# Attention steps moved in a fused attention and mixture-of-experts kernel: reciprocals' division, values' and Q's projections, norm, rank and split at other steps

## The chip, the cores and the metric

The kernel runs on one core of a Trainium2 chip. The metric is the device time of one execution in microseconds, the median of several. Engines are named as in the profile: PE (TensorE, with PEld for its weight loads), DVE (VectorE), ACT (ScalarE), POOL (GpSimd), SP (SyncE, which only issues DMAs here).

## The reference

Input x is 16 batches of 512 tokens with 256 channels.

```python
q, k, v = heads(wq, bq), heads(wk, bk), heads(wv, bv)     # 16 heads of 16
q, k = rope(q), rope(k)
att = softmax(causal(q @ k.T * 0.25))
x = layernorm(x + (att @ v) @ wp.T + bp)
probs = softmax(x @ gate_w.T)                              # 32 experts
top_w, top_idx = top_k(probs, 8); top_w /= top_w.sum()
y = sum over chosen e of top_w[e] * ((u * silu(g)) @ down_w[e].T),  g, u = split(x @ gate_up_w[e].T)
out = layernorm(x + y)
```

## The kernel before

It has two phases. In the attention phase the main loop runs over i, the batch (0 to 15), and e, a step (0 to 31). Eight steps are one group of four heads; k = e % 8 is the place in the group. At each step PE computes two scores (`score`, lines 1075 and 1077: keys by queries, then a mask), ACT takes their exponentials (`exp`), and PE multiplies these with the values at odd steps (`pv`, line 1089). Beside this run, at steps that the table `SLOT_...` gives, three other jobs:

- For batch i + 1: transposes of x, projections of Q, K and values (`p1_qk`, line 1024; `p1_v`, line 1035), rope on DVE (line 1634) and its rotation (`rotate`, 1641 and 1642), and the split of Q and K into three bfloat16 parts: ACT copies a part (`part_copy`, tile pbuf), DVE subtracts (`rest`, 1650; `last_part`, 1657). ACT puts the values into vx (`values`). SP writes the parts to DRAM and loads them back in other order (tile stacks).
- For the group after next: row maxima of the scores. PE computes them in eleven units (`max_unit`, 1049 and 1051), at the (k, place) pairs of `PLACES`, and DVE reduces each (`reduce_unit`, 1664).
- For batch i - 1, its end: SP fetches the softmax sums (tile den), DVE takes reciprocals, SP writes them out (step 6) and reads them back broadcast over 16 rows (`reciprocals_in`, step 10, tile xTden) after the numerators (step 9, tile ynum; it waits for the rotation of K). DVE divides (`divide`, 1927), PE projects (`project`, 1100 and 1102, steps 15 and 16), DVE adds (1818) and takes statistics (1825, 1828; steps 16 and 17). GpSimd computes the inverse root (`rsqrt`, 872 and 874), DVE the mean column (1835), ACT the norm (tile x), GpSimd stores it (878). Then transposes, router, choice, ranks, and GpSimd's scatter of batch i - 2's rows (888) by expert, 32 per batch at steps 0 to 19.

Each step of PE has three places for such jobs: 0 after the first score, 1 and 2 after the second and `pv`. Every engine works through its own queue in the order that this loop writes; semaphores tie the queues. All jobs with an output in PSUM outside scores share four banks in turn (`odd_plan` and the class `Odd`): a job waits until the reader of the job four before it is done. `odd_plan` repeats the loop to number them, which is why the change touches both.

In the second phase PE computes the experts (152 steps k, two blocks of 256 rows each), ACT and DVE copy the results, and GpSimd scatters them to token order (`rows_to_tokens`, 906, four per step; buffers for seven blocks). The end of batch 15 runs at the same step numbers of this phase, so `SLOT_RSQRT` and others apply there too. GpSimd also scatters the rows of batches 14 and 15 (888). DVE sums each token's eight rows at the end.

Of the kernel before, what the change touches and what calls it, by code (L numbers as in the profile page):

```python
# [37 lines left out]

SLOT_X = (0, 1)
SLOT_Q = (2, 3)  # L40
SLOT_V = (5, 7)
SLOT_K = (6, 7)
SLOT_X_OUT = (0, 1)
SLOT_ROPE_Q = (2, 3)
SLOT_ROPE_K = (6, 7)
SLOT_VALUES = (5, 6)
SLOT_ROTATE = (3, 7)
SLOT_FIRST = (4, 9)
SLOT_REST = (4, 9)
SLOT_SECOND = (5, 10)  # L50
SLOT_LAST = (5, 11)
SLOT_WRITE = (7, 12)
SLOT_DEN = 2
SLOT_RECIP = 4
SLOT_REC_OUT = 6
SLOT_REC_IN = 10
SLOT_NUM = 9
SLOT_DIVIDE = 12
SLOT_PROJECT = (15, 16)
SLOT_ADD = (15, 16)  # L60
SLOT_STATS = (16, 17)
SLOT_RSQRT = 20
SLOT_MEAN = 20
SLOT_NORM = 22
SLOT_STORE = 21
SLOT_X1 = (24, 25)
SLOT_X1_OUT = (24, 25)
SLOT_SPLIT = 26
SLOT_LOWER = 29
SLOT_ROUTER = 26  # L70
SLOT_ROUTER_IN = 26
SLOT_CHOICE = (26, 27)
SLOT_MASK = 27
SLOT_RANK = 28
SLOT_RANK_IN = 28
SLOT_EXP = 28
SLOT_RESIDUAL = 0
SCATTER_STEPS = 20
SLOT_WEIGHTS = 31
SLOT_TABLE = 10  # L80
SLOT_TABLE_OUT = 25
SLOT_TAILS = 27

STEPS = 32
LE = STEPS // NQ

PLACES = [(4, 0), (5, 1), (6, 0), (6, 2), (7, 0), (7, 1), (7, 2), (0, 1), (1, 0), (1, 1), (1, 2)]
MSLOT = {at: m for m, at in enumerate(PLACES)}
MHALF = 4
SPLIT, TURN, TURN_OUT, ROWS_K = (1, 2), (3, 2), 3, 4  # L90
# [183 lines left out]
def odd_plan():  # L274

    bank, at = {}, [0]

    def take(i, *job):
        bank[job] = 6 if i >= B else 3 + at[0] % 4
        at[0] += 1  # L280
    for kc in range(NC):
        take(0, "x", 0, kc)
    for n in range(2):
        for half in range(2):
            take(0, "qk", 0, n, half)
    for v in range(2):
        take(0, "v", 0, v)
    for m in range(NM):
        take(0, "max", 0, m)
    take(0, "turn", 0)  # L290
    for m, (k, place) in enumerate(PLACES):
        if k >= MHALF:
            take(0, "max", 1, m)
    for i in range(B + 2):
        for e in range(STEPS):
            g, k = e // LE, e % LE
            end, nxt = 1 <= i <= B, i <= B - 2
            for place in range(3):
                if place == 0 and e == SLOT_TABLE_OUT and table_of(i - 1):
                    take(i, "table", i - 1)  # L300
                if place == 1:
                    if e in SLOT_X and nxt:
                        take(i, "x", i + 1, SLOT_X.index(e))
                    if e in SLOT_Q and nxt:
                        take(i, "qk", i + 1, 0, SLOT_Q.index(e))
                    if e in SLOT_K and nxt:
                        take(i, "qk", i + 1, 1, SLOT_K.index(e))
                    if e in SLOT_V and nxt:
                        take(i, "v", i + 1, SLOT_V.index(e))
                    if e in SLOT_PROJECT and end:  # L310
                        take(i, "project", i - 1, SLOT_PROJECT.index(e))
                    if e in SLOT_X1 and end:
                        take(i, "x1", i - 1, SLOT_X1.index(e))
                    if e == SLOT_ROUTER and end:
                        take(i, "router", i - 1)
                if place == 2 and e == SLOT_RANK and end:
                    take(i, "rank", i - 1)
                n = max_group(i, e)
                if n is not None:
                    if (k, place) in MSLOT:  # L320
                        take(i, "max", n, MSLOT[k, place])
                    if (k, place) == TURN:
                        take(i, "turn", n)
            if prep_step(i, e):
                stage, p = prep_step(i, e)
                if p + E * stage in range(1, E + 1):
                    take(i, "gu", p + E * stage - 1)
                    take(i, "dn", p + E * stage - 1)
                if stage == 1 and p in (2, 3):
                    take(i, "fin", p - 2)  # L330
    return bank
# [9 lines left out]
def build(nc, x, wq, bq, wk, bk, wv, bv, wp, bp, gate_w, gate_up_w, down_w,  # L341
# [9 lines left out]
    with ExitStack() as ctx:  # L351
# [601 lines left out]
        def _(pe):  # L953
# [59 lines left out]
            def p1_transpose(b, kc):  # L1013
                wait(pe, s_xin, 16 * (b + 1))
                k = odd.take(s_xT, 2 * b + kc + 1, "x", b, kc)
                xpose4(k, lambda n: xin[:, n, kc * P:(kc + 1) * P]).then_inc(s_p1t, 1)

            def p1_qk(b, n, half):

                wait(pe, s_xT, 2 * b + 2)  # L1020
                w = (wqT, wkT)[n]
                k = odd.take(s_rope, 8 * b + 4 * n + 2 * half + 2, "qk", b, n, half)
                for kc in range(NC):
                    last = mmul(ps[:, k, :], w[:, kc, half * P:(half + 1) * P], xTden[:, kc, :],  # L1024
                                start=(kc == 0), stop=(kc == NC - 1))
                last.then_inc(s_p1q, 1)

            def p1_v(b, v):

                wait(pe, s_xT, 2 * b + 2)  # L1030
                k = odd.take(s_vx, 2 * b + v + 1, "v", b, v)
                for m in range(2):
                    t = 2 * v + m
                    for kc in range(NC):
                        last = mmul(ps[:, k, m * C:(m + 1) * C], xTden[:, kc, t * P:(t + 1) * P], wvT[:, kc, :],
                                    start=(kc == 0), stop=(kc == NC - 1))
                last.then_inc(s_p1v, 1)
# [68 lines left out]
            def x1_transpose(b, kc):  # L1106
                wait(pe, s_x1, NT * (b + 1))
                k = odd.take(s_x1T, 2 * b + kc + 1, "x1", b, kc)
                xpose4(k, lambda n: x1[:, n, kc * P:(kc + 1) * P]).then_inc(s_x1t, 1)
# [104 lines left out]
            def odd_job(i, e, place):  # L1214

                end, nxt = has(i, 1, NB), has(i, 0, NB - 2)
                if place == 0 and e == SLOT_TABLE_OUT:
                    for t in table_of(i - 1):
                        table_transpose(t)
                if place == 1:  # L1220
                    if e in SLOT_X and nxt:
                        p1_transpose(i + 1, SLOT_X.index(e))
                    if e in SLOT_Q and nxt:
                        p1_qk(i + 1, 0, SLOT_Q.index(e))
                    if e in SLOT_K and nxt:
                        p1_qk(i + 1, 1, SLOT_K.index(e))
                    if e in SLOT_V and nxt:
                        p1_v(i + 1, SLOT_V.index(e))
                    if e in SLOT_PROJECT and end:
                        project(i - 1, SLOT_PROJECT.index(e))  # L1230
                    if e in SLOT_X1 and end:
                        x1_transpose(i - 1, SLOT_X1.index(e))
                    if e == SLOT_ROUTER and end:
                        router(i - 1)
                if place == 2 and e == SLOT_RANK and end:
                    rank(i - 1)

                k, n = e % LE, max_group(i, e)
                if n is not None:
                    if (k, place) in MSLOT:  # L1240
                        max_unit(n, MSLOT[k, place])
                    if (k, place) == TURN:
                        max_transpose(n)
# [303 lines left out]
        def _(dve):  # L1547
# [133 lines left out]
            def router_in(b):  # L1681
                wait(dve, s_gt, b + 1)
                V.tensor_copy(lg[:, :, :], ps[:, odd_bank("router", b), 0:NT * E].rearrange("p (t e) -> p t e", t=NT)).then_inc(s_rt, 1)
# [262 lines left out]
            def odd_job(i, e, place):  # L1946

                end, nxt = has(i, 1, NB), has(i, 0, NB - 2)
                if place == 0 and e == SLOT_TABLE_OUT:
                    for t in table_of(i - 1):  # L1950
                        table_out(t)
                if place == 1:
                    if e in SLOT_ROPE_Q and nxt:
                        rope(i + 1, 0, SLOT_ROPE_Q.index(e))
                    if e in SLOT_ROPE_K and nxt:
                        rope(i + 1, 1, SLOT_ROPE_K.index(e))
                    if e in SLOT_ADD and end:
                        ln_add(i - 1, SLOT_ADD.index(e))
                    if e == SLOT_ROUTER_IN and end:
                        router_in(i - 1)  # L1960
                if place == 2 and e == SLOT_RANK_IN and end:
                    rank_in(i - 1)
                k, n = e % LE, max_group(i, e)
                if n is not None:
                    if (k, place) in MSLOT:
                        reduce_unit(n, MSLOT[k, place])
                    if (k, place) == SPLIT:
                        split_max(n)
# [131 lines left out]
```

## Time and profile before

| | us |
|---|---|
| median of 3 runs | 2179.51 (2176.76 to 2180.5) |
| profiled execution | 2177.83 |
| its span | 2175.9 |
| PE busy | 1805.7 (83%) |
| DVE busy | 1601.1 (74%) |
| ACT busy | 1356.5 (62%) |
| POOL busy | 1245.6 (57%) |

Busy shares are means over two phases with different limits, so they say little by themselves. The issue time of DMAs is not in them. A row with an idle time in brackets says how long the engine stood before that instruction and what ended it.

### The profile page before, as it was taken

The page shows a single profiled execution, that of the slowest core. Times are in us where ns is not written, and L with a number is a line of the kernel's source. Part 1 is how long each engine was busy: PE and PEld are TensorE (multiplying, and loading weights), DVE is VectorE, ACT ScalarE, POOL GpSimd, SP SyncE. Part 2 cuts the span into 40 slices and gives each one's busy share as a digit, 9 for nine tenths or more (in the row PEclk, how much of TensorE's full clock was granted, in tenths as well). Part 3 has the DMA queues.
Part 4 walks back from the last instruction along what each step waited for, and adds up shares of the span by engine and source line. Part 5 has one row for each costly group of instructions (what it writes and reads, how often), then busy time and mean ns, then how long its engine had stood idle before and what let it go on. Part 6 is the DMA issues. An engine that isn't in the chain of part 4 may idle for free.

```text
span 2175.9 us, 54014 instructions
## 1 busy us (share of the span) xinstructions
PE 1805.7 (83%) x17104; PEld 1295.0 (60%) x17104; DVE 1601.1 (74%) x3572; ACT 1356.5 (62%) x3265; POOL 1245.6 (57%) x1206
## 2 busy tenths in 40 slices
PE   4899888998888888988878988899888889988920
PEld 2555554555555544555445877788777678777820
DVE  4888787877888778877864545475456677778988
ACT  1657565666565555555445867788777678888820
POOL 1004356444644465445543777777777777777860
PEclk8999999999999999999988999999999999999965
DMA  5456567666756766566676765656689889989977
GB/s 142 120 153 196 190 215 228 199 199 209 235 184 198 254 212 204 172 192 210 197 228 235 243 201 189 204 191 211 201 299 299 304 295 308 300 285 356 356 237 251
DMA packets 242891, 495.04 MB, mean 228 GB/s; under 512 B 47800, under 2 KB 140415, under 8 KB 232848
## 3 DMA queue, kind: packets, MB, share of 16 engines
q1 hardware_dynamic: 158720, 299.30, 44.4%
q0 software_dynamic: 58368, 163.70, 20.4%
q10 hardware_dynamic: 25536, 28.58, 3.9%
q8 instruction: 155, 2.54, 0.5%
q14 instruction: 112, 0.92, 0.1%
HBM read 284.54 MB, written 234.04 MB: 238 GB/s over the span
## 4 chain that ended last, share of the span: by engine, by line
PE 40%; DVE 19%; DMA 14%; issue 11%; ACT 7%; POOL 5%; SPq 2%; ACTq 1%; POOLq 0%; DVEq 0%
DMA xTden<-reciprocals 6%; DVE mn L1664 5%; PE ps L1024 4%; POOL y_tokens L906 4%; PE ps L1102 3%; DMA y_tokens<-work,yidx 3%; PE ps L1049 3%; PE ps L1163 3%; PE ps L1075 3%; PE ps L1143 3%; PE ps L1145 3%; PE ps L1144 3%; PE ps L1089 3%; PE ps L1209 2%; PE ps L973 2%
## 5 line engine op out<-in xcount | busy, mean ns | idle before, releaser
L1301 ACT ACTIVATE pT<-ps 128x512 f32<-128x512 f32 (+2 forms) x1008 | 677.7, 703 | 381.8 <-PE ps L1077 292.6
L888 POOL DMA_INDIRECT x_sorted<-xhl,idx x512 | 529.2, 1034 | 483.6 <-DVE xhl L1739 229.4
L1664 DVE TENSOR_REDUCE mn<-ps 128x1 f32<-128x512 f32 (+3 forms) x704 | 412.9, 632 | 51.0 <-PE ps L1051 48.6
L1143 PE MATMUL ps<-pT,gu_hi 128*128 128x256 f16 (+1 forms) x1600 | 371.0, 251 | 43.2 <-ACT pT L1301 43.0
L1144 PE MATMUL ps<-pT,gu_hi 128*128 128x256 f16 (+1 forms) x1600 | 370.0, 250 | 0.0
L1145 PE MATMUL ps<-pT,gu_lo 128*128 128x256 f16 (+1 forms) x1600 | 369.7, 250 | 0.0
L906 POOL DMA_INDIRECT y_tokens<-work,yidx x264 | 279.5, 1059 | 79.8 <-issue 61.2
L1049 PE MATMUL ps<-stacks 96*128 96x512 bf16 (+3 forms) x1024 | 273.8, 310 | 42.5 <-DVE mn L1664 25.6
L1075 PE MATMUL ps<-stacks 99*128 99x512 bf16 (+3 forms) x1024 | 283.7, 308 | 15.4 <-ACT pT L1301 12.3
L1077 PE MATMUL ps<-maskk,identb 128*128 128x128 bf16 x1024 | 221.8, 222 | 0.0
L1209 PE MATMUL ps<-dn,vx 128*128 x608 | 168.5, 277 | 53.2 <-DVE cosT L1872 15.5
L1051 PE MATMUL ps<-maskq,identb 128*128 128x128 bf16 x1024 | 198.5, 224 | 0.0
L1089 PE MATMUL ps<-pT,vx 128*32 128x512 f32 (+3 forms) x2048 | 195.5, 454 | 2.8 <-ACT pT L1301 2.6
L1143 PEld LDWEIGHTS ps<-pT,gu_hi 128*128 x1600 | 158.2, 99 | 64.9 <-issue 52.0
L1049 PEld LDWEIGHTS ps<-stacks 96*128 96x128 bf16 x1024 | 102.3, 100 | 129.2 <-DVE mn L1664 50.1
L1858 DVE TENSOR_TENSOR vx<-vx 128x512 f16<-128x512 f32 x152 | 105.0, 691 | 99.8 <-ACT vx L1301 98.6
L1211 PE MATMUL ps<-dn,vx 128*128 x608 | 169.2, 278 | 0.0
L1210 PE MATMUL ps<-dn,vx 128*128 x608 | 168.9, 278 | 0.0
L1145 PEld LDWEIGHTS ps<-pT,gu_lo 128*128 x1600 | 158.3, 99 | 11.4
L1144 PEld LDWEIGHTS ps<-pT,gu_hi 128*128 x1600 | 158.6, 99 | 7.6
L1075 PEld LDWEIGHTS ps<-stacks 99*128 99x128 bf16 x1024 | 102.5, 100 | 101.2 <-ACT pT L1301 26.2
L1853 DVE SCALAR_TENSOR_TENSOR vx<-vx,ps 128x512 f32<-128x512 f32 x152 | 103.8, 683 | 61.8 <-PE ps L1145 60.0
(255 smaller groups left out, 3899.3 us busy)
## 6 DMA issues: line engine op xcount, KB each, us to landing
stacks<-y_tokens SPq DMA_DIRECT2D x64, 1024.0 KB
stacks<-qk_parts SPq DMA_DIRECT2D x128, 192.0 KB
qk_parts<-pbuf SPq DMA_DIRECT2D x31, 768.0 KB, 4.4
stacks<-qk_parts SPq DMA_DIRECT2D x128, 128.0 KB
attention<-yev ACTq DMA_DIRECT2D x64, 256.0 KB
stacks<-x_sorted SPq DMA_DIRECT2D x52, 304.0 KB, 4.2
x_sorted<-pads_h SPq DMA_DIRECT2D x99, 152.0 KB
pbuf<-x_sorted SPq DMA_DIRECT2D x40, 304.0 KB
```

What stands on the lines that cost most here:

```text
L888: pool.indirect_dma_start(xsort[g][:, :], bass.IndirectOffsetOnAxis(ap=at, axis=0), xhl_rows[:, t, :], None).then_inc(s_scat, 16)
L906: pool.indirect_dma_start(ytok[g][:, :], bass.IndirectOffsetOnAxis(ap=yidx[:, c:c + 1], axis=0), ysb[n % NYR][:, m, :].bitcast(I32), None, ...
L1049: mmul(ps[:, k, a * n:(a + 1) * n], qs[0:KS, r, h, tt * P:(tt + 1) * P], ks[0:KS, r, h, 0:n], start=True, stop=False)
L1075: mmul(ps[:, o, at:at + n], ks[0:KX, r, h, s * P:(s + 1) * P], qs[0:KX, r, h, s * P:T], start=True, stop=False)
L1077: last = mmul(ps[:, o, at:at + P], identb[:, :], maskk[:, :], start=False, stop=True)
L1089: last = mmul(ps[32 * j:32 * j + 32, BANK_PV, s * P:T], value_columns(i % 2, s, 4 * g + j), pT[s % 2][:, j, 0:T - s * P], start=(s == 0), ...
L1143: mmul(o, w_hi[k], x_hi[k], start=k == 0, stop=False)
L1144: mmul(o, w_hi[k], x_lo[k], start=False, stop=False)
L1145: last = mmul(o, w_lo[k], x_hi[k], start=False, stop=k == n - 1)
L1209: mmul(o, h_hi, d_hi, start=True, stop=False)
L1301: return nc.scalar.activation(o, i, f, **k)
L1664: V.tensor_reduce(mn[:, tt, h0:h0 + nh], ps[:, odd_bank("max", at, m), 0:nh * n].rearrange("p (a n) -> p a n", a=nh), axis=AX.X, op=ALU.ma ...
```

## The change

It changes step numbers (`SLOT_...`), adds a place within the step for each of the jobs of PE and of their readers on DVE (`PLACE_...`, where before all had place 1 and rank had 2), and moves one maximum unit from (5, 1) to (5, 0). No instruction is added or removed.

```diff
-SLOT_V = (5, 7)
+SLOT_V = (6, 8)
-SLOT_VALUES = (5, 6)
+SLOT_VALUES = (5, 8)
-SLOT_FIRST = (4, 9)
+SLOT_FIRST = (4, 8)
-SLOT_DEN = 2
+SLOT_DEN = 1
-SLOT_DIVIDE = 12
+SLOT_DIVIDE = 13
-SLOT_RSQRT = 20
+SLOT_RSQRT = 16
-SLOT_STORE = 21
+SLOT_STORE = 20
-SLOT_SPLIT = 26
+SLOT_SPLIT = 28
-SLOT_RANK = 28
-SLOT_RANK_IN = 28
+SLOT_RANK = 29
+SLOT_RANK_IN = 29
+PLACE_X = (1, 1)
+PLACE_Q = (0, 0)
+PLACE_V = (0, 0)
+PLACE_K = (1, 1)
+PLACE_ROPE_Q = (0, 1)
+PLACE_ROPE_K = (1, 1)
+PLACE_PROJECT = (1, 1)
+PLACE_ADD = (1, 1)
+PLACE_X1 = (1, 1)
+PLACE_ROUTER = 1
+PLACE_ROUTER_IN = 1
+PLACE_RANK = 0
+PLACE_RANK_IN = 0
-SLOT_TAILS = 27
+SLOT_TAILS = 26
+def due(e, place, slots, places):
+    return e in slots and place == places[slots.index(e)]
-PLACES = [(4, 0), (5, 1), (6, 0), (6, 2), (7, 0), (7, 1), (7, 2), (0, 1), (1, 0), (1, 1), (1, 2)]
+PLACES = [(4, 0), (5, 0), (6, 0), (6, 2), (7, 0), (7, 1), (7, 2), (0, 1), (1, 0), (1, 1), (1, 2)]
```

In `odd_plan` and in `odd_job` of PE and DVE each test changes in the same manner, for example:

```diff
-                if place == 1:
-                    if e in SLOT_Q and nxt:
-                        p1_qk(i + 1, 0, SLOT_Q.index(e))
+                if due(e, place, SLOT_Q, PLACE_Q) and nxt:
+                    p1_qk(i + 1, 0, SLOT_Q.index(e))
-                if place == 2 and e == SLOT_RANK and end:
+                if (e, place) == (SLOT_RANK, PLACE_RANK) and end:
                     rank(i - 1)
```

## Rows read from the trace of the kernel before

**Rows 1.** Of the page: busy time of each engine; TensorE's granted clock in 40 slices.
```profile
PE 1805.7 (83%) x17104; PEld 1295.0 (60%) x17104; DVE 1601.1 (74%) x3572; ACT 1356.5 (62%) x3265; POOL 1245.6 (57%) x1206
...
PEclk8999999999999999999988999999999999999965
```

**Rows 2.** All waits: who waited for whom; us in total, times, longest.
```profile
PE ps L1100 <- DVE mn L1664: 45.3, 15, 7.5
...
DVE ynum L1927 <- DMA xTden<-reciprocals: 40.6, 15, 8.1
...
ACT vx L1301 <- PE ps L1035: 86.9, 15, 5.8
...
DVE tiny L1835 <- POOL tiny L874: 18.8, 7, 13.0
...
PE ps L973 <- ACT work L1301: 26.0, 17, 1.9
...
PE ps L1024 <- DVE mn L1664: 10.1, 17, 0.9
```

**Rows 3.** Chain that ended last, 498 to 514 us (batch 6): start, us, what.
```profile
497.98 0.61 DVE qf L1642
...
500.63 0.57 SPq L714
...
501.25 9.21 DMA xTden<-reciprocals
...
511.78 0.61 DVE mn L1664
```

**Rows 4.** Timeline, batch 6, 480 to 530 us: start, us, engine, line, operation [idle before].
```profile
484.09 0.75 DVE L1634 SCALAR_TENSOR_TENSOR qf<-ps,bqc,cosT 128x512 f32<-128x512 f32 x1 [0.94 <-PE ps L1024]
...
489.28 1.06 ACT L1301 ACTIVATE pbuf<-qf 128x1024 bf16<-128x1024 f32 x1 [0.39 <-DVE qf L1650]
...
494.21 1.89 PE L1035 MATMUL ps<-wvT,xTden 128*128 128x256 f32 x8
...
496.36 1.02 DVE L1664 TENSOR_REDUCE mn<-ps 128x1 f32<-128x384 f32 x2 [0.39 <-PE ps L1051]
...
510.49 1.29 DVE L1927 TENSOR_TENSOR ynum<-ynum,xTden 128x512 f32<-128x512 f32 x2 [2.92 <-DMA xTden<-reciprocals]
```

**Rows 5.** First projection: TensorE's timeline in batches 3 and 6; windows of line 1102.
```profile
296.35 0.27 PE L1100 MATMUL ps<-spare,ones 65*128 65x256 bf16 x1 [1.78 <-DVE mn L1664]
...
296.46 1.03 PE L1102 MATMUL ps<-wpT,ynum 128*128 128x256 f32 x4
...
512.53 0.37 PE L1100 MATMUL ps<-spare,ones 65*128 65x256 bf16 x1 [2.37 <-DVE mn L1664]
...
512.69 1.92 PE L1102 MATMUL ps<-wpT,ynum 128*128 128x256 f32 x4
...
152.60:156.60 4.00, 2.96 (x12) 2.11 (x13) 1.00 0.60 149
...
512.60:516.60 4.00, 3.60 (x8) 2.33 (x8) 0.58 0.71 228
```

**Rows 6.** Timeline of GpSimd and VectorE, batch 6, at the norm.
```profile
520.03 0.97 POOL L888 DMA_INDIRECT x_sorted<-xhl,idx  x1 [0.49 <-PE ps L1077]
...
524.74 0.25 DVE L1828 BATCH_NORM_AGGREGATE mv<-st 128x2 f32<-128x6 f32 x2
...
525.73 0.19 POOL L872 TENSOR_SCALAR tiny<-mv 128x4 f32<-128x4 f32 x1
```

**Rows 7.** Experts' phase: GpSimd's largest group, 1185 to 2110 us; timelines 1276 to 1312.
```profile
L906 POOL DMA_INDIRECT y_tokens<-work,yidx x264 | 279.5, 1059 | 79.8 <-issue 61.2
...
1279.09 0.25 DVE L1828 BATCH_NORM_AGGREGATE mv<-st 128x2 f32<-128x6 f32 x2
...
1282.89 0.97 POOL L888 DMA_INDIRECT x_sorted<-xhl,idx  x1 [0.30 <-issue]
...
1308.74 0.16 DVE L1835 SCALAR_TENSOR_TENSOR tiny<-mv,tiny 128x4 f32<-128x4 f32 x1 [12.99 <-POOL tiny L874]
```

More of the change, by code:

```diff
@@ L300, in odd_plan @@
                     take(i, "table", i - 1)
-                if place == 1:
-                    if e in SLOT_X and nxt:
-                        take(i, "x", i + 1, SLOT_X.index(e))
-                    if e in SLOT_Q and nxt:
[L305 to L315, printed above, removed]
-                if place == 2 and e == SLOT_RANK and end:
+                if due(e, place, SLOT_X, PLACE_X) and nxt:
+                    take(i, "x", i + 1, SLOT_X.index(e))
+                if due(e, place, SLOT_Q, PLACE_Q) and nxt:
+                    take(i, "qk", i + 1, 0, SLOT_Q.index(e))
+                if due(e, place, SLOT_K, PLACE_K) and nxt:
+                    take(i, "qk", i + 1, 1, SLOT_K.index(e))
+                if due(e, place, SLOT_V, PLACE_V) and nxt:
+                    take(i, "v", i + 1, SLOT_V.index(e))
+                if due(e, place, SLOT_PROJECT, PLACE_PROJECT) and end:
+                    take(i, "project", i - 1, SLOT_PROJECT.index(e))
+                if due(e, place, SLOT_X1, PLACE_X1) and end:
+                    take(i, "x1", i - 1, SLOT_X1.index(e))
+                if (e, place) == (SLOT_ROUTER, PLACE_ROUTER) and end:
+                    take(i, "router", i - 1)
+                if (e, place) == (SLOT_RANK, PLACE_RANK) and end:
                     take(i, "rank", i - 1)
@@ L1219, in odd_job @@
                         table_transpose(t)
[L1220 to L1223, printed above, removed]
-                        p1_qk(i + 1, 0, SLOT_Q.index(e))
[L1225 to L1235, printed above, removed]
+                if due(e, place, SLOT_X, PLACE_X) and nxt:
+                    p1_transpose(i + 1, SLOT_X.index(e))
+                if due(e, place, SLOT_Q, PLACE_Q) and nxt:
+                    p1_qk(i + 1, 0, SLOT_Q.index(e))
+                if due(e, place, SLOT_K, PLACE_K) and nxt:
+                    p1_qk(i + 1, 1, SLOT_K.index(e))
+                if due(e, place, SLOT_V, PLACE_V) and nxt:
+                    p1_v(i + 1, SLOT_V.index(e))
+                if due(e, place, SLOT_PROJECT, PLACE_PROJECT) and end:
+                    project(i - 1, SLOT_PROJECT.index(e))
+                if due(e, place, SLOT_X1, PLACE_X1) and end:
+                    x1_transpose(i - 1, SLOT_X1.index(e))
+                if (e, place) == (SLOT_ROUTER, PLACE_ROUTER) and end:
+                    router(i - 1)
+                if (e, place) == (SLOT_RANK, PLACE_RANK) and end:
                     rank(i - 1)
@@ L1951, in odd_job @@
                         table_out(t)
[L1952 to L1961, printed above, removed]
+                if due(e, place, SLOT_ROPE_Q, PLACE_ROPE_Q) and nxt:
+                    rope(i + 1, 0, SLOT_ROPE_Q.index(e))
+                if due(e, place, SLOT_ROPE_K, PLACE_ROPE_K) and nxt:
+                    rope(i + 1, 1, SLOT_ROPE_K.index(e))
+                if due(e, place, SLOT_ADD, PLACE_ADD) and end:
+                    ln_add(i - 1, SLOT_ADD.index(e))
+                if (e, place) == (SLOT_ROUTER_IN, PLACE_ROUTER_IN) and end:
+                    router_in(i - 1)
+                if (e, place) == (SLOT_RANK_IN, PLACE_RANK_IN) and end:
                     rank_in(i - 1)
```

## The prediction

> **What bounds the kernel now.** I read the page first: TensorE is busy 83% of the span and its clock falls to half again and again [rows 1]. Two phases follow from the slices: sixteen attention batches up to about 1170 us, then the experts. Next I read the waits. In attention the longest wait of TensorE is one place, the first projection of a batch (line 1100), 45.3 us in 15 times, 3.0 us each; VectorE waits 40.6 us for the broadcast reciprocals just before it [rows 2]. Then the chain of waits over one batch: the rotation of K ends at 498.6, SyncE issues numerators and reciprocals, the reciprocals' DMA takes 9.21 us, the two divisions follow, then one maximum of 0.61 us, and only then the projection starts at 512.53 [rows 3 to 5]. So an attention batch is paced by this chain: rotation, DMA, division, projection.
>
> The experts' phase has another bound. Its GpSimd scatter of results takes 1.06 us each with 0.30 us before it, 608 of them and 63 row scatters, without a hole from 1183 to 2107 (the largest group is in [rows 7]): 264 take 279.5 + 79.8 us, so 1.36 us each, and 608 of them at that price are 827 us, the row scatters some 80 more. What other engines lose there costs nothing while GpSimd is busy.
>
> **The change part by part.** Nothing is added or removed; instructions change their place in each queue. The times are of the profiled execution, 2177.8 us (its span 2175.9 and 1.9 around it); the median of the runs shown is 1.7 above it.
>
> Division from step 12 to the end of 13. TensorE's first projection (step 15) needs both the division and the maximum of step 13, whose bank it takes. Before, VectorE waits 2.92 us for the DMA, divides, and does that maximum last (0.61 us, [rows 3, 4]). After, the maximum lies in the wait, since its matmuls are done early (they move to place 0 of step 5 of each group as well), and the division comes last. Gain: one maximum a batch, 15 x 0.61 = 9 us. Where there is no DMA wait (batches 8 and 14, which compute tables) the sum of the two is the same and the gain is nothing, so 13 to 15 times: 8 to 9 us. Nothing behind the division suffers: the maxima of step 14 are needed only after the projection, which takes over 2 us.
>
> Values' projection. Its second half moves from step 7, behind K's second half and ahead of two maxima, to step 8. Before, VectorE idles 0.39 us for the maxima behind the 1.89 us of matmul, and these stand ahead of K's rotation [rows 4]. That 0.39 goes. ScalarE, which sat up to 5.8 us for this half (86.9 us in all, [rows 2]), no longer does; but that idle time hid nothing that TensorE waited for, as TensorE ran its own queue meanwhile, so I give it nothing. The first half moves behind a maximum and a score, so it ends some 0.4 us later.
>
> Q's projection to place 0 of steps 2 and 3. The second half then runs ahead of a score and of a product with the values. VectorE idles 0.94 us before that rope [rows 4] and starts sooner by at most that. But ScalarE copies the second part of Q (489.28, [rows 4]) behind the evacuation of the values' first half, which is now later by 0.4; before, it left 0.39 idle there. So of 0.94 about 0.2 arrives. Together K's rotation ends 0.4 to 0.7 us sooner. How much of this reaches the division depends on the DMA: between 0 and 0.7, and I take 0.4, since stack loads of the same queue still run when the numerators are issued. Fourteen batches: 6 us (0 to 10).
>
> At this place a rule of the Trainium skill speaks against the change. The page "DMA: Bandwidth & Descriptors", section "Queues, rings and completion order", says that each engine consumes descriptors of one queue in ring order, so that what is issued sooner on SyncE's queue still stands behind the stack loads issued ahead of it. By that rule the landing moves only as the loads do, 0.2 us a batch, and this term would be 3 us and not 6. The row shows only that the DMA takes 9.21 us from the last issue, not what it stands behind [rows 3].
>
> The clock. When TensorE has waited for the projection, the next matmuls run at the lower level: 1.92 us for four in batch 6, after 2.37 us of waiting, against 1.03 in batch 3, which had waited 1.78 us only [rows 5]. Of the 15 windows laid from each first projection over 4 us, 13 have a mean granted clock of 0.50 to 0.64 and two have 1.00 (the first and the sixth are in [rows 5]); one of the two is the batch that had waited 1.78 us. Four matmuls lose 0.9 us; the eight of this projection lose at most 1.8 and, as the clock came back within them, some 1.6 us. If the wait shrinks by 1.0 us (0.6 + 0.4), the batches that waited 2.1 to 2.4 us, five of them by the timeline (batch 6 is the row), come near the 1.8 that kept the clock. I take four that keep it: 4 x 1.6 = 6 us (0 to 13 x 1.6 = 21).
>
> Norm: rsqrt on GpSimd from step 20 to 16. The scatters of steps 17 to 19, four of them, now stand behind its wait for the statistics. In batch 6 GpSimd is at step 17's scatter near 520 and the statistics end at 525.0 [rows 6]; so GpSimd idles over 5 us and the four scatters (0.97 us and 0.30 ahead of each) end near 532, instead of 525.7. Their reader is the split, which moves from 26 to 28, some 5 us behind that, and the store stands at 20, behind the norm; the slack covers both. If it did not, a late split costs up to 1 us a batch. The mean column waits for rsqrt 5.8 us in seven late batches (of 18.8 us, the other 13.0 lies in the experts' phase, [rows 2, 7]); this goes. I take half as passed on: 3 us (0 to 6).
>
> Rank moves by a score (0.2 us), VectorE's ropes and ScalarE's early copy of K's part by a step, all with their producers: 0, bounds -3 to +3 us from the shortest waits near them. The softmax sums' fetch at step 1 instead of 2 gives nothing: SyncE has nothing between, and it waits for ScalarE's store at its own step 2. The table's tails move by one step: nothing waits.
>
> Experts' phase. There rsqrt at 20 holds VectorE 12.99 us (1308.74, [rows 7]). The statistics are ready at 1279.34. GpSimd would reach step 16 at about 1284, behind the row scatter of step 15 at 1282.89, so it doesn't wait, and VectorE's 13 us go. But GpSimd was busy through them, and it bounds this phase: gain 0 to 1 us, a loss up to 3 if the store at 20 must wait for the norm at 22. I take 0.
>
> Sum: 9 + 6 + 6 + 3 + 0 = 24 us. 2177.8 - 24 = 2153.8, and at the level of the median 2155.
>
> **The rivals.** (B) Only the reordering counts: the DMA lands as before and the clock stays low. Gain 9 us, 2170. For it: the loads on the same queue; by the rule above it would be a little more, 2168. Against: VectorE's and the loads' start move too. Chance 0.17.
>
> (C) The wait goes altogether: TensorE's projection wait of 45.3 us and the low clock behind it, 13 x 1.6 = 21 us, less what other waits take over (a third): 66 x 2/3 = 44 us, 2135, at the full 66 us 2113. For it: batch 3, with a wait of 1.8 us, kept its clock. Against: my gain of 1.0 us is a third of the mean wait. Chance 0.15.
>
> (D) The gain turns into another wait, within 0.2% of before: 2178. For it: TensorE waits 26.0 us in 17 times for scaled weights, and 10.1 for maxima [rows 2]; a sooner start meets these. Chance 0.11.
>
> (E) Slower. The early copy of K's part (1.06 us for one such copy, [rows 4]) with the values' evacuation now stands on ScalarE ahead of the exponentials of step 9, and the score of step 10 needs one of these. I work out that it is ready some 0.9 us after TensorE comes there. This decides if TensorE's time up to the projection, not the chain, ends last: then it is 0.9 x 15 = 13 us on top, 2191. Against: 3.0 us of waiting at the projection absorb it. Chance 0.10.
>
> The forecast itself has 0.47. Its own range is 2143 to 2168. The range for 8 in 10 reaches into (C) and to the edge of (D): 2122 to 2180. A difference of 0.2%, 4.4 us, is about what runs can tell. Faster: 0.47 + 0.17 + 0.15 = 0.79, less 0.02 for (B) at its end: 0.77; same 0.13; slower 0.10.
>
> **What would show it.** Right: the maximum of step 13 stands ahead of the division and the projection follows the division within 0.2 us; line 1100's wait falls from 45.3 to about 30 us; more of the 15 windows have a clock near 1.00; ScalarE's wait for the values' projection nearly vanishes; VectorE's 13 us in the experts' phase vanish and that phase keeps its length. Wrong: the reciprocals' DMA grows by what its issue gains (B); a new wait of 0.9 us at the score of step 10 without a fall at line 1100 (E); the split waits for scatters; the wait at line 1100 is gone in most batches (C).

## The result: 25 us faster, most of what the traces show ahead of the first projection

| us | before | after |
|---|---|---|
| median (lowest to highest, runs) | 2178.14 (2166.42 to 2180.5, 4) | 2153.03 (2144.49 to 2157.7, 4) |
| profiled execution | 2177.83 | 2157.70 |
| its span | 2175.9 | 2155.8 |

The ratio is 0.9891, its 95% interval 0.9843 to 0.9938. Lines of the code stand 17 or 18 further down in the kernel after: the projection of lines 1100 and 1102 is at 1118 and 1120, the maximum at 1681, the division at 1944, rsqrt at 890 and 892, the mean column at 1852, and the row scatter at 906 (a number that `rows_to_tokens` had before).

The page of the kernel after, with the rows that answer to [rows 1]:

```profile
PE 1812.3 (84%) x17104; PEld 1297.4 (60%) x17104; DVE 1598.4 (74%) x3572; ACT 1364.2 (63%) x3265; POOL 1243.9 (58%) x1206
...
PEclk8999999999999999999989999999999999999965
```

The busy times moved by less than 8 us each; the time went out of idle stretches. The windows of the two phases say in which phase. Columns: the stretch, its length, busy time with counts of PE, PEld, DVE, ACT and POOL, then the mean clock. Kernel before (first score of batch 1 is at 115.9, last score at 1172.5):

```profile
60.00:1172.50 1112.50, 974.31 (x7841) 576.86 (x7838) 890.58 (x2158) 635.65 (x1241) 509.06 (x507) 0.95 0.62 199
1172.50:2108.40 935.90, 800.74 (x9125) 698.47 (x9123) 623.10 (x1233) 706.99 (x2004) 721.27 (x686) 0.96 0.79 265
```

Kernel after, the same two phases:

```profile
58.90:1154.90 1096.00, 976.93 (x7871) 578.25 (x7869) 891.52 (x2164) 645.47 (x1246) 508.78 (x507) 0.95 0.63 203
1154.90:2089.80 934.90, 805.66 (x9125) 701.49 (x9123) 624.04 (x1235) 707.92 (x2005) 720.38 (x687) 0.96 0.79 265
```

The last score of attention comes 17.6 us sooner, the experts' phase is 1.0 shorter, the sums behind it 1.5. In attention the mean clock has not moved, and neither have the busy times, but for ScalarE's, which is 10 us longer.

The waits of the kernel after, the rows that answer to [rows 2]:

```profile
POOL tiny L890 <- DVE mv L1845: 121.7, 15, 42.4
DVE ynum L1944 <- DMA xTden<-reciprocals: 38.1, 12, 7.8
PE ps L1118 <- issue: 37.7, 12, 7.0
PE ps L991 <- ACT work L1318: 25.8, 17, 1.9
ACT vx L1318 <- PE ps L1053: 15.7, 15, 1.2
...
DVE tiny L1852 <- POOL tiny L892: 3.4, 6, 1.4
PE ps L1042 <- DVE mn L1681: 3.4, 15, 0.6
PE ps L1118 <- DVE ynum L1944: 2.8, 2, 1.7
```

The wait at the projection is now in two rows, 37.7 + 2.8 = 40.5 us; it was 45.3. TensorE's wait at K's banks (line 1042, before 1024) went from 10.1 to 3.4, ScalarE's for the values from 86.9 to 15.7, the mean column's from 18.8 to 3.4. GpSimd now waits at rsqrt, 121.7 us: 42.4 of it once, in batch 1, where it stood 43.3 us before as well, and some 5.5 us in each later batch.

The chain of the last end does not pass through batch 6 in this execution, so I show the same stretch by the timeline, as [rows 4 and 5] did for before. Batch 6 begins (first score) at 472.9 before and at 471.6 after, 1.3 us sooner:

```profile
494.93 0.68 DVE L1658 TENSOR_TENSOR qf<-qf,ynum 128x512 f32<-128x512 f32 x1
495.53 0.68 DVE L1659 TENSOR_TENSOR qf<-qf,ynum 128x512 f32<-128x512 f32 x1
...
496.24 1.34 SPq L739 DMA_DIRECT2D ynum<-attention  x2
497.74 2.15 SPq L732 DMA_DIRECT2D xTden<-reciprocals  x2
...
504.86 1.31 DVE L1681 TENSOR_REDUCE mn<-ps 128x1 f32<-128x512 f32 x2 [0.23 <-PE ps L1069]
...
509.01 1.29 DVE L1944 TENSOR_TENSOR ynum<-ynum,xTden 128x512 f32<-128x512 f32 x2 [2.84 <-DMA xTden<-reciprocals]
510.23 1.74 DVE L1681 TENSOR_REDUCE mn<-ps 128x1 f32<-128x512 f32 x3
...
510.41 0.27 PE L1118 MATMUL ps<-spare,ones 65*128 65x256 bf16 x1 [2.10 <-issue]
```

From the start of the division to the projection it is now 1.40 us, where it was 2.04 (510.49 to 512.53, [rows 4, 5]): the maximum of 0.61 us no longer stands between. The rotation of K ends at 24.6 us of the batch, not 25.7.

For the whole phase I worked the same distances out of one trace of each run, as means over batches 1 to 15 in us from the batch's first score (the rotation over 14); e1 to e12 are the experiments below. "Issued" is the end of the last of the four issues of numerators and reciprocals on SyncE, "rest" runs from the projection's first weighted matmul to the next batch, "low" is the time in us in these batches at the lower of the two clock levels.

```
               rotation issued division projection rest   low
before          25.61   28.35   36.78    39.10    31.34   102
e1              25.61   28.31   36.93    38.46    31.44    85
e3              25.61   28.29   36.78    39.08    31.33    99
e2              24.39   27.23   36.07    38.36    31.08    96
after           24.39   27.37   36.30    37.89    31.31   102
e10 (= after)   24.38   27.15   36.05    37.58    30.96    82
e4              24.69   27.51   36.29    37.81    30.93    79
e11 (= e4)      24.69   27.52   36.35    37.88    31.07    89
e5              25.15   27.94   36.51    38.03    30.73    61
e8              24.39   27.26   36.14    38.16    29.90    48
e9              24.69   27.57   36.39    38.33    30.08    58
e6              24.38   26.03   35.52    37.05    30.31    58
e12             24.39   25.91   35.67    37.82    30.07    48
e7              24.39   25.58   33.94    35.67    29.94    44
```

Before to after: the projection comes 1.21 us sooner, times 15 is 18 us; the rest and the low time are the same. That is the whole 17.6 us of the phase (batch 1 begins 1.0 later). A second trace of the kernel after (e10) has the projection 1.52 us and the rest 0.38 us shorter than before, so one pair of traces fixes these differences only to some 0.3 us a batch.

### The profile page after: what moved, and what is told of

The parts are those of the page before. It is cut to its first block and busy times, and to the rows that moved or that the text cites. A ratio compares the mean times of both kernels' runs of the same rounds, so it can differ in the third digit from the quotient of the medians.

```text
span 2155.8 us, 54014 instructions
## 1 busy us (share of the span) xinstructions
PE 1812.3 (84%) x17104; PEld 1297.4 (60%) x17104; DVE 1598.4 (74%) x3572; ACT 1364.2 (63%) x3265; POOL 1243.9 (58%) x1206
## 5 line engine op out<-in xcount | busy, mean ns | idle before, releaser
L1681 DVE TENSOR_REDUCE mn<-ps 128x1 f32<-128x512 f32 (+3 forms) x704 | 415.0, 632 | 45.3 <-PE ps L1069 42.9
L1093 PE MATMUL ps<-stacks 99*128 99x512 bf16 (+3 forms) x1024 | 295.3, 308 | 11.5 <-ACT pT L1318 6.8
L1163 PEld LDWEIGHTS ps<-pT,gu_lo 128*128 x1600 | 159.0, 99 | 11.2
```

The source lines that it names most:

```text
L1093: mmul(ps[:, o, at:at + n], ks[0:KX, r, h, s * P:(s + 1) * P], qs[0:KX, r, h, s * P:T], start=True, stop=False)
L1163: last = mmul(o, w_lo[k], x_hi[k], start=False, stop=k == n - 1)
L1681: V.tensor_reduce(mn[:, tt, h0:h0 + nh], ps[:, odd_bank("max", at, m), 0:nh * n].rearrange("p (a n) -> p a n", a=nh), axis=AX.X, op=ALU.ma ...
```

## The experiments

Theory 1: an attention batch is paced by rotation of K, issue on SyncE, DMA of the reciprocals, division, projection. Theory 2, the rival: TensorE's other waits, which the moved projections of Q and values shorten, are what the change saved. The clock was a question of its own. Three groups ran on a chip each, with the kernel before beside them: e1 to e4; e5, e7, e8 and e9; e6, e10, e11 and e12. The medians of before there: 2180.32 (20 runs), 2178.63 (11), 2177.91 (11). Behind each median stand its range and number of runs, then the ratio to before with its 95% interval.

**e1, the division alone**, in the kernel before:

```diff
-SLOT_DIVIDE = 12
+SLOT_DIVIDE = 13
```

> The kernel before with the division at step 13 and nothing else. Theory 1 (the chain rotation, DMA, division, projection paces a batch): the maximum of step 13 goes into the DMA wait, 0.6 us a batch, 8 to 9 us faster than before, about 2169. Theory 2 (the gain of the change comes from waits of TensorE for exponentials and for K's bank, which went down by 12 us in the trace after, and the projection's wait is only what is left over): no change, within 3 us of before.

Measured: 2168.26 (2161.78 to 2175.19, 9); 0.9949, 0.9931 to 0.9967. 12 us. The distance from division to projection falls by the table from 2.32 to 1.53 us, 15 times 0.8 = 12. In this trace the division itself starts 0.15 us later, so the projection comes 0.64 us sooner, 10 us in all, and batches 1 to 15 take 8 us less. The prediction's largest term is shown, at 8 to 12 where it said 9. The wait at the projection, in the waits of e1:

```profile
PE ps L1100 <- issue: 35.1, 13, 7.0
```

**e2, the change without the division's move:**

```diff
-SLOT_DIVIDE = 13
+SLOT_DIVIDE = 12
```

> The kernel after with the division back at step 12. Theory 1: 8 to 9 us slower than after, about 2162. Theory 2: the time of after, 2153, within 3 us.

Measured: 2160.42 (2156.47 to 2166.23, 6); 0.9908, 0.9887 to 0.9929: 7 us behind the kernel after. That compares two chips; by the ratios to before the edit is worth 2 to 4 us (0.9891 and 0.9898 against 0.9908). By the table the projection is 0.47 us later than in the kernel after, 7 us in all. So from this side the division is worth 2 to 7 us, from e1 it was 8 to 12: its gain is shown, its size only roughly, and the 9 lies between. The wait at the projection has its old releaser again, in the waits of e2:

```profile
PE ps L1118 <- DVE mn L1681: 46.6, 16, 7.0
DVE ynum L1944 <- DMA xTden<-reciprocals: 44.5, 15, 7.7
```

The same run says what all the other parts are worth together: 20 us against before on the same chip (2180.32 to 2160.42), of which the table has 11 in the earlier projection and 4 in the shorter rest. From e1 to the kernel after, which differ by the same parts, it is 13 to 15 us (2168.26 to 2155.48, that is e10, or 2153.03). The prediction had 6 + 6 + 3 = 15 for them.

**e3, the norm's steps alone**, in the kernel before:

```diff
-SLOT_RSQRT = 20
+SLOT_RSQRT = 16
-SLOT_STORE = 21
+SLOT_STORE = 20
-SLOT_SPLIT = 26
+SLOT_SPLIT = 28
```

> The kernel before with rsqrt at 16, store at 20 and split at 28 alone. Theory 1: the chain does not hold it, so 1 to 3 us faster than before (the store's wait of 0.8 us and part of 5.8 us of VectorE's waits); VectorE's wait of 13.0 us in the experts' phase goes and gives nothing there, as GpSimd is without a hole. Rival: that wait was on the path, then 10 to 13 us faster. If the scatters behind rsqrt come late for the split: slower by up to 15 us.

Measured: 2177.01 (2170.43 to 2181.3, 12); 0.9985, 0.997 to 1.0. That is 3 us, with an interval that ends at none; the profiled execution shows no gain in attention (the table). VectorE's 13 us at the mean column are gone here too, in the waits of e3:

```profile
DVE tiny L1835 <- POOL tiny L874: 3.4, 6, 1.4
```

So that gap was not worth the 10 to 13 us of the rival; at most it is part of these 3 us, and the interval ends at 7.

**e4, the change with the values' projection as it was:**

```diff
-SLOT_V = (6, 8)
+SLOT_V = (5, 7)
-SLOT_VALUES = (5, 8)
+SLOT_VALUES = (5, 6)
-SLOT_FIRST = (4, 8)
+SLOT_FIRST = (4, 9)
-PLACE_V = (0, 0)
+PLACE_V = (1, 1)
-PLACES = [(4, 0), (5, 0), ...
+PLACES = [(4, 0), (5, 1), ...
```

> The kernel after with the values' projection, its evacuation, the copy of K's part and the maximum unit back at their old steps; division, Q and norm stay moved. Theory 1: K's rotation ends about 0.5 us later in the batch, 5 to 9 us slower than after, about 2160. Theory 2: the waits for exponentials at steps 11 and 13 and for K's bank come back, 12 us slower, about 2165, and the projection's wait falls by as much as those rise.

Measured: 2141.73 (2136.61 to 2157.55, 6); 0.9833, 0.9801 to 0.9865. Not slower, as both theories had it, but 11 us ahead of the kernel after. ScalarE's long wait is back and costs nothing:

```profile
ACT vx L1318 <- PE ps L1053: 99.2, 30, 6.0
```

TensorE's waits for exponentials rise too, by 8.4 us. The rotation is only 0.3 us later (the table). I took the 11 us as a question of spread, since the kernel after had been timed on another chip, and ran both again as e10 and e11.

**e5, the change with Q's projection as it was:**

```diff
-PLACE_Q = (0, 0)
+PLACE_Q = (1, 1)
-PLACE_ROPE_Q = (0, 1)
+PLACE_ROPE_Q = (1, 1)
```

> The kernel after with Q's projection and its rope back at place 1; all else as after. Theory 1: 0.94 us of VectorE's idle time comes back, of which 0.2 us a batch reaches K's rotation: 0 to 3 us slower than after. Theory 3 (Q's earlier place is what brings K's rotation forward by 1.0 us in the batch, as it came 0.8 us earlier still with the values' projection at its old steps): rotation 0.8 us later in each batch and 8 to 12 us slower than after.

Measured: 2152.8 (2143.64 to 2159.39, 6); 0.9876, 0.9843 to 0.9909: the time of the kernel after. TensorE's wait at K's banks is back at 9.6 us, and so is the idle time before Q's rope (first row; second, the later rotation), in e5's batch 6, which begins at 467.5:

```profile
478.73 0.75 DVE L1651 SCALAR_TENSOR_TENSOR qf<-ps,bqc,cosT 128x512 f32<-128x512 f32 x1 [0.92 <-PE ps L1042]
...
491.44 0.68 DVE L1658 TENSOR_TENSOR qf<-qf,ynum 128x512 f32<-128x512 f32 x1
```

By the table the rotation is 0.76 us later, the division only 0.2 to 0.5 and the projection 0.1 to 0.45 (against after and e10), so 2 to 7 us were to be lost; the spread of the runs covers that. A low time of 61 us in this execution goes the other way. So this run neither shows a loss nor excludes one of that size.

**e7, the reciprocals' DMAs (two a batch) taken out of the kernel after.** It leaves the normalisation by the softmax sums out: nothing is loaded into xTden and the division doesn't wait for it.

```diff
-                for c in range(NC):
-                    src = rec_dram[b][8 * c:8 * c + 8, :].rearrange("h (o t) -> h o t", o=1).to_broadcast([8, D, T])
-                    sp.dma_start(xTden[:, c, :], src).then_inc(s_yd, 16)
...
-                wait(dve, s_yd, 64 * (b + 1))
+                wait(dve, s_yd, 32 * (b + 1))
```

> The kernel after without the broadcast of the reciprocals to tile xTden: SyncE does not issue it, the division waits for the numerators alone and multiplies by what lies in xTden, so that the attention's result is not normalised (left out: 2 DMAs a batch). Theory 1: the projection's wait of 40 us and the low clock behind it go, 35 to 60 us faster than after, about 2105. Rival (the wait is cover for the maxima, VectorE ends last): under 15 us faster, 2140.

Measured: 2105.04 (2104.66 to 2107.33, 4); 0.9661, 0.9628 to 0.9694. 48 us ahead of the kernel after. In its batch 6 the division has no idle time before it (first fence), and in the whole run it waits for the numerators once, in batch 15 (second fence, of the waits):

```profile
491.26 1.28 DVE L1941 TENSOR_TENSOR ynum<-ynum,xTden 128x512 f32<-128x512 f32 x2
```

```profile
DVE ynum L1941 <- DMA ynum<-attention: 3.3, 1, 3.3
PE ps L1115 <- DVE ynum L1941: 2.9, 2, 1.7
```

This settles the bound: the broadcast of the reciprocals holds 48 of the 2153 us. By the table the earlier projection is 29 to 33 us of it and the shorter rest, with a low time of 44 us, 15 to 21; what follows attention is the same within 2 us. The four runs also lie within 2.7 us of each other, where those of the kernel after span 13 to 15. That suggests that the spread comes with this wait; four runs don't show it.

**e8, sixteen idle matmuls ahead of the projection's wait**, in the kernel after, so that TensorE is not at rest there:

```diff
+FILL = 16
...
+                k = odd.take(s_ln1, LN * b + v + 1, "project", b, v)
+                for f in range(FILL if v == 0 else 0):
+                    mmul(ps[:, k, 0:C], ones[0:65, :], biasp[0:65, :], start=True, stop=True)
                 wait(pe, s_yn, 2 * b + 2)
-                k = odd.take(s_ln1, LN * b + v + 1, "project", b, v)
```

> The kernel after with 16 idle matmuls (65 rows, 256 columns, 0.11 us each, overwritten by the projection) at the first projection of each batch, ahead of the wait for the division. Clock theory: TensorE's clock no longer falls there in most batches, 1.6 us a batch in 13 batches less 1.7 us in the three batches without a long wait: 10 to 18 us faster than after, about 2140. Rival (the fall of the clock is not set by this wait but by what went before it, so the filler changes nothing of it): 0 to 5 us slower than after.

Measured: 2148.1 (2145.29 to 2152.52, 4); 0.986, 0.9825 to 0.9895. 5 us ahead of the kernel after (standard error 2.4), fewer than expected. The clock did what it should: ten of the 15 windows at the first projection have 1.00, where the kernel after has two and e10 four, and the four matmuls behind the fill take 1.03 us, those of the kernel after took 1.07 and then 1.91. In e8, batch 6 (which begins at 464.5):

```profile
501.18 1.92 PE L1117 MATMUL ps<-spare,ones 65*128 65x256 bf16 x16
501.62 1.29 DVE L1947 TENSOR_TENSOR ynum<-ynum,xTden 128x512 f32<-128x512 f32 x2 [2.51 <-DMA xTden<-reciprocals]
...
503.10 1.03 PE L1123 MATMUL ps<-wpT,ynum 128*128 128x256 f32 x4
```

In the kernel after, batch 6:

```profile
510.52 1.07 PE L1120 MATMUL ps<-wpT,ynum 128*128 128x256 f32 x4
...
511.59 1.91 PE L1120 MATMUL ps<-wpT,ynum 128*128 128x256 f32 x4
```

By the table the low time falls from 82 to 102 us to 48 and the rest of a batch from 31.0 to 31.3 us to 29.9, some 16 to 21 us in all. But the distance from division to projection grows from 1.5 to 2.0 us (7 us), since TensorE is often still in the fill when the division is done; the projection is 0.3 to 0.6 us later in the batch (4 to 9 us). And the profiled execution of the kernel after that had the lower low time (e10) needs only 7 us more in these batches (1028.1 against 1021.0).

**e9, e4 with the fill of e8:**

> The kernel with the values' projection back at its old steps (2141.7 us measured) and the same 16 idle matmuls. Clock theory: the difference between that kernel and after, 11 us, is the clock (its trace has 78 us at the low level in batches 1 to 15, after has 102); with the filler both kernels come to the same time within 4 us, about 2135. Rival (it is the order of the work that makes the difference): the 11 us stay between them, 2130 against 2140 or 2142 against 2153.

Measured: 2146.23 (2136.94 to 2150.51, 5); 0.9832, 0.9801 to 0.9863. It comes within 2 us of e8, as the clock theory had it, though both at 2147 and not at 2135. It is also within the spread of e4: the fill and the values' old place do not add up.

**e10, the kernel after once more, and e11, e4 once more**, on one chip:

> The kernel after itself, on the same chip as the next three, since the kernels were so far compared over different chips. It should come to 2153 (ratio 0.989) within its interval; what the next three are worth is read against this one.

> The kernel after with the values' projection at its old steps, once more. If the 11 us that it was ahead of after are real (the move of the values' projection costs): 8 to 14 us faster than after on this chip. If they are the spread of the clock between executions (the rotation of K is only 0.3 us later in its batches and the first projection starts at the same place): within 5 us of after, either way.

Measured: e10 2155.48 (2143.84 to 2159.23, 6); 0.9898, 0.9875 to 0.9921. e11 2151.4 (2144.96 to 2156.03, 6); 0.9874, 0.985 to 0.9898. The 11 us shrink to 4, with intervals that overlap. All 10 runs of the kernel after have the mean 2153.2 (standard error 1.8), all 12 with the values back 2147.8 (2.0). So the values' move gives nothing, and may cost up to some 10 us; which of the two stays open. Theory 2 has e4, e5 and e11 against it: e4 and e11 bring ScalarE's wait and TensorE's for exponentials back, e5 TensorE's at K's banks, and none is slower. All of them back at once is e1, and there the same 13 to 15 us are missing that theory 1 gives to rotation, clock and norm; so the theories are told apart by e1, the single edits and e7, not by that sum.

**e6, reciprocals read back ahead of the numerators**, in the kernel after. In its batch the numerators (issued at the end of rotation, which frees their tile) stand ahead of the reciprocals in SyncE's queue, though xTden is free sooner:

```diff
-SLOT_REC_IN = 10
+SLOT_REC_IN = 9
```

> The kernel after with the reciprocals' read-back issued at step 9, ahead of the numerators instead of behind them; it needs K's and the values' projections only and not K's rotation. Chain theory: SyncE's last issue for the division comes 1.4 us sooner in each batch, of which 0.5 to 1.4 reaches the projection: 7 to 20 us faster than after, about 2141. Rival (the queue of SyncE drains in order and is full, so the last landing is where it was): within 4 us of after, the DMA's wait grows by what the issue gains.

Measured: 2133.2 (2128.32 to 2137.39, 5); 0.9796, 0.9771 to 0.9821. 22 us ahead of the kernel after on the same chip, and the best whole version of this study. In its batch 6 (begins at 456.1):

```profile
479.66 1.32 SPq L732 DMA_DIRECT2D xTden<-reciprocals  x2
480.05 0.68 DVE L1659 TENSOR_TENSOR qf<-qf,ynum 128x512 f32<-128x512 f32 x1
...
481.08 1.59 SPq L739 DMA_DIRECT2D ynum<-attention  x2
...
492.25 1.29 DVE L1944 TENSOR_TENSOR ynum<-ynum,xTden 128x512 f32<-128x512 f32 x2 [1.17 <-DMA ynum<-attention]
...
493.64 0.27 PE L1118 MATMUL ps<-spare,ones 65*128 65x256 bf16 x1 [0.94 <-issue]
...
493.75 1.03 PE L1120 MATMUL ps<-wpT,ynum 128*128 128x256 f32 x4
```

The reciprocals are under way before the rotation ends; the last issue ends at 26.6 us of the batch, not 28.3; the division's idle time falls from 2.84 to 1.17, and now the numerators end it. The waits of e6:

```profile
PE ps L1118 <- issue: 21.3, 12, 3.5
DVE ynum L1944 <- DMA ynum<-attention: 18.9, 12, 4.3
```

By the table the projection is 0.5 to 0.8 us sooner a batch than in e10 and after (8 to 13 us) and the rest 0.65 to 1.0 us shorter (10 to 15 us), as the low time goes from 82 to 102 us to 58: in batch 6 the matmuls after a wait of 0.94 us keep the full level, and nine of the 15 windows at the first projection have 1.00, where e10 has four.

**e12, e6 with the fill of e8:**

> The same with the 16 idle matmuls ahead of the projection's wait. Chain theory with the clock: the wait is now near the filler's 1.7 us, so the clock stays in most batches: 10 to 25 us faster than after, about 2135, and 0 to 8 us faster than without the filler. Rival: the filler now delays the projection in the batches whose wait is shorter than it, and the kernel is 0 to 5 us slower than without it.

Measured: 2137.06 (2129.57 to 2139.61, 5); 0.9801, 0.9777 to 0.9826. No gain: low time 48 instead of 58 us, but 2.15 instead of 1.5 us from division to projection. Where the wait is short, the fill only stands in the way.

## Why the prediction was right, and where its terms were not

**The bound** was read rightly: chain of rotation, issue, DMA, division, projection. e7 takes one link out and the batch loses 48 us.

**The division, 9 us.** Right: the maximum stands ahead of it, the projection follows 0.1 us behind its end; 8 to 12 us in e1, 2 to 7 in e2. Batches 8 and 14, which the prediction left out, had waits of 0.41 and 0.33 us for the DMA before.

**Values and Q, 6 us.** The sum was about right and both steps of it were off. "K's rotation ends 0.4 to 0.7 us sooner" was 1.22 (25.61 to 24.39). The step that failed is Q's, "of 0.94 about 0.2 arrives": in e5 undoing it alone moves the rotation by 0.76. Counted from the first score, the rope of Q's second half began 1.2 us sooner in batch 6 (484.09 - 472.9 = 11.2, and 481.56 - 471.6 = 10.0), more than the idle time shown before it, and the wait for ScalarE that I feared took 0.7 of it: 0.86 us of idle time before the last part, which had 0.18. So 0.6 us of Q's gain went through, and the 0.39 us before the maxima, which went as forecast, came on top. In the kernel after:

```profile
481.56 0.74 DVE L1651 SCALAR_TENSOR_TENSOR qf<-ps,bqc,cosT 128x512 f32<-128x512 f32 x1
...
488.56 1.23 DVE L1674 TENSOR_TENSOR pbuf<-qf,pbuf 128x1024 bf16<-128x1024 f32 x1 [0.86 <-ACT pbuf L1318]
```

Values back moves the rotation by 0.3. Of the 1.22 the issues kept 0.98 and the start of the division 0.48: from the last issue's end to the division it takes 8.93 us instead of 8.43. In e10 the issues kept 1.20 and the division 0.73. So rival B's mechanism, a DMA that grows by what its issue gains, held for 0.5 us a batch, about half. 0.48 to 0.73 us times 15 is 7 to 11 us, beside my 6.

The rule of the Trainium skill, "DMA: Bandwidth & Descriptors", section "Queues, rings and completion order", spoke for 3 us, 0.2 a batch, as by it the earlier issue stands behind the same loads. The division moved by more than twice that, so the measurement decides against the 3 us; what the DMA stood behind no trace here shows. Undone singly, neither part shows a loss in the time (e5, e11). Undone together, with the clock and the norm, they are the 13 to 20 us of e1 and e2; how these divide is read from the traces alone.

**The clock, 6 us: not in the profiled execution, and in the mean open.** "I take four that keep it" failed there; of the 15 windows two kept it, as before. In e10, the same kernel, four did, and the rest of a batch is 0.38 us shorter than before, 6 us in all. The mean granted clock that every run has on record was 0.938 in 42 runs of before and 0.941 in the 10 of the kernel after (standard error 0.001). Over an execution that is an estimated 13 us less at the lower level, worth 5 us at the 0.4 below. So part of the term probably came, and by luck of the execution the profile shows none.

The step behind the count was wrong too: that a wait near 1.8 us keeps the clock. By the trace four batches of before had waited 2.1 to 2.4 us, not five, and batch 14 had waited only 1.38 and has 0.50. In the kernel after, batch 8 waited 1.09 us at the projection and its window has 0.50 as well, but TensorE had stood 2.61 us for maxima just ahead of that (columns of the last row: stretch, length, PE, PEld, clock):

```profile
647.67 0.34 PE L1067 MATMUL ps<-stacks 96*128 96x384 bf16 x1 [2.61 <-DVE mn L1681]
...
650.41 0.37 PE L1118 MATMUL ps<-spare,ones 65*128 65x256 bf16 x1 [1.09 <-DVE ynum L1944]
...
650.40:654.40 4.00, 3.81 (x8) 2.40 (x8) 0.50 0.76 202
```

So this one wait does not decide the level by itself. Kernel after, windows of line 1120 from the first projection of batches 1 and 6 (columns: stretch, length, PE, PEld, clock):

```profile
155.40:159.40 4.00, 2.00 (x8) 1.36 (x8) 1.00 0.44 117
510.50:514.50 4.00, 2.98 (x8) 1.81 (x8) 0.61 0.79 237
```

The wait didn't shrink by what the projection gained, because TensorE came earlier as well: its waits at K's banks fell by 6.7 us, those for exponentials by 7.9. Batch 6 waited 2.10 us, not 2.37. The expected fall of the wait from 45.3 to 30 was one to 40.5 (37.6 to 38 in e10). The price was about right: over the fourteen traces the rest of a batch follows the low time, (31.3 - 29.9) x 15 = 21 us for 102 - 48 = 54 us, 0.4 us for each us at the lower level. The 102 us before are 20 stretches, so 2 us a stretch, where I had 1.6 a batch.

**The norm, 3 us:** e3 measured 3, barely told from none, and its trace shows no gain. GpSimd waits 5.50 us at rsqrt in batch 6, as worked out; the scatters end near 530 and nothing waits for them. Timeline of the kernel after, answering to [rows 6]:

```profile
522.92 0.19 POOL L890 TENSOR_SCALAR tiny<-mv 128x4 f32<-128x4 f32 x1 [5.50 <-DVE mv L1845]
...
528.58 0.97 POOL L906 DMA_INDIRECT x_sorted<-xhl,idx  x1 [0.30 <-issue]
```

**The experts' phase, 0:** right. The mean column has no idle time (12.99 in [rows 7]), GpSimd goes on without a hole, and the phase is 934.9 us long after 935.9. Kernel after:

```profile
1281.59 0.15 DVE L1852 SCALAR_TENSOR_TENSOR tiny<-mv,tiny 128x4 f32<-128x4 f32 x1
```

**The rest at 0** stays so: no wait of the rank, table or softmax sums' fetch is in the list. **Rival E** did not appear: no wait at the score of step 10. **Rival C** needed the DMA gone.

The sum by the traces: division 11 (2.32 to 1.59 us), rotation and DMA 7, clock 0, batch 1's later start -1, experts' phase and end 2.5: 20 us, the difference of the two spans. Of the medians it is 25 us, 5 more than these two executions; the profiled run of the kernel after was the slowest of its four. That the forecast of 24 met the 25 is in part luck: the division and the chain gave more than their 15 us, clock and norm gave nothing in these traces where 9 stood, and the experts' phase and the end gave 2.5 where nothing stood.

## What to carry to other kernels

Find the chain that releases the engine, and put only what that chain needs between its last transfer and that engine; work that is ready goes into the wait (e1). Then look at the issuing queue: a transfer that could start but stood behind one that must wait was worth 22 us here for one step number, against 7 to 11 for making its neighbours earlier. An engine's shorter wait elsewhere brings it to the next one earlier, so the wait that you watch shrinks less than the time does.

## What the runs showed of the hardware

- The time at the lower clock level differs between executions of one kernel, 102 and 82 us in attention, and the times spread by 13 to 15 us; without the wait for the reciprocals four runs spread by 2.7 us.
- Keeping TensorE busy through the wait halved the low time (48 us) but gave 5 us, not the 16 to 21 of the shorter rest of the batch; the later projection took 4 to 9 of them back.
- With the last issue's end 1.0 to 1.2 us sooner (kernel after and e10), the division that waits for the DMA began 0.5 to 0.7 us sooner; with the issues in another order and their end another 1.1 to 1.3 us sooner (e6), it began another 0.5 to 0.8 sooner.
- The level of the clock behind a wait does not follow that wait alone: 0.50 after 1.09 us (batch 8 of the kernel after) and after 1.38 us (batch 14 of before), 1.00 after 1.78 us (batch 3 of before).
